# The flow layer's first stage put in batch order, its weights issued by the scalar engine, its first table load on a constant

## The chip, the cores and the metric

The kernel runs on one NeuronCore of a Trainium2 chip. Its engines are TensorE (PE, matrix products; PEld is its weight load), VectorE (DVE), ScalarE (ACT), GpSimd (POOL) and SyncE (SP), which here only issues transfers. Each engine runs its own list of instructions in order, and they meet through semaphores. The metric is the device time of one execution in microseconds.

## The reference, cut to what matters

Two layers of attention and feed-forward work on 2 x 1024 tokens of width 128. What the change touches is the beginning of the first one, a "flow" attention with 16 heads of 8:

```
x = L0_attn_inputs                                # (2, 1024, 128)
u = layernorm(x)
q = sigmoid(u @ Wq + bq); k = sigmoid(u @ Wk + bk); v = u @ Wv + bv
normal   = 1, 2, ..., L
sink_in  = normal / sum_d((q + EPS) * (cumsum(k) + EPS))
src_out  = normal / sum_d((k + EPS) * (cumsum(q) + EPS))
cons_sink = sum_d((q + EPS) * (cumsum(k * src_out) + EPS)) / normal
cons_src  = clip(sum_d((k + EPS) * (cumsum(q * sink_in) + EPS)) / normal, -1, 1)
sink_alloc = sigmoid(cons_sink)
e = exp(cons_src); src_comp = e / cumsum(e) * normal
x = einsum(q * sink_in / normal, cumsum(k (x) (v * src_comp))) * sink_alloc
```

After it come the output projection, a feed-forward part, a gated attention (8 heads of 64), a second attention (16 heads of 8) and a layer of experts. None of these is edited.

## The kernel before, in words

The kernel is a chain of blocks; at the end of each block all engines meet. The change is inside one block of `flow_phase`, the first, called "mass" (lines 282 to 600), and every later block starts after it.

The 2048 tokens are cut into four quarters of 512 (`QUARTERS`), each of four tiles of 128; quarters 0 and 1 are batch 0, quarters 2 and 3 are batch 1 (`PERB` is 2). A quarter goes through these steps:

- SP loads it (L334), one transfer of 256 KB.
- DVE takes mean and variance of its tiles (`quarter_stats`, L106 and L109), ACT takes the root (`quarter_root`, L117), DVE takes the reciprocal and applies both (`quarter_norm`, L124 and L127).
- PE turns it so that channels lie in the partitions (L466, four transposes against the constant `ident`).
- ACT copies the turned quarter as its high part (`quarter_high`, L144), DVE subtracts for the low part (`quarter_low`, L148).
- PE projects it (`project(m, q)`, m = 0, 1, 2 for q, k, v), three matmuls for each (L71 to L73), and ACT adds the bias and takes the sigmoid into `qT`, `kT` or `vT` (`activate`, L554). `PROJ` (L315) numbers the twelve projections; a projection waits until the one four before it was read.

POOL splits the weights into high and low parts (L156, L158) once all three have landed. From line 426 on DVE runs one long chain in which each instruction waits for the one before it (`done`, L362): running sums (`scan`, L371), products (`weigh`, L374), and shares by head. The head sums (L481) and their spreading back (L491) are small matmuls, the batches taken in turn. `fill` (L76) issues matmuls of the identity in bf16 whose result nobody reads.

The order on each engine is written out by hand. On PE (L495 to L505) and on ACT (L557 to L572) it is: batch 0 turned, its k and q projected, batch 1 turned, its k and q, then the four v. On DVE the statistics of a quarter, the norm of the one before and the low part of the one before that alternate (L414 to L421).

Of the kernel before, what the change touches and what calls it, by code (L numbers as in the profile page):

```python
# [64 lines left out]
def tile(t):  # L65
    return slice(t * P, (t + 1) * P)
# [184 lines left out]
def flow_phase(nc, psum, X, C, io, const, lead):  # L251
# [9 lines left out]
    with ExitStack() as ctx:  # L261
# [20 lines left out]
        with ExitStack() as ctx1:  # L282
# [7 lines left out]
            small = p1.sb("small", [P, 1])  # L290
            q_more, k_more = p1.sb("q_more", [P, SEQ]), p1.sb("k_more", [P, SEQ])
# [10 lines left out]
            x_loaded = [p1.sem(f"x_loaded{q}") for q in range(QUARTERS)]  # L302
            ident_loaded, w_loaded, bias_loaded = p1.sem("ident_loaded"), p1.sem("w_loaded"), p1.sem("bias_loaded")
# [26 lines left out]
            def _(sp):  # L330
# [4 lines left out]
                for n, name in enumerate(("Wq", "Wk", "Wv")):  # L335
                    sp.dma_start(w_raw[:, tile(n)], io[f"L0_attn_{name}"]).then_inc(w_loaded, 16)
                sp.dma_start(C["ident"], const["ident"]).then_inc(ident_loaded, 16)
# [21 lines left out]
            def _(dve):  # L359
# [31 lines left out]

                def allot(b):

                    dve.wait_ge(alloc_ready, b + 1)
                    done(dve.tensor_tensor(r_sink[:, b, :], r_sink[:, b, :], alloc[:, b, :], ALU.mult))
                    dve.wait_ge(exp_ready, b + 1)
                    done(dve.tensor_tensor_scan(cum_give[:, b, :], give[:, b, :], give[:, b, :], 0.0, ALU.add, ALU.bypass), f"cum_give{b}")
                    done(dve.tensor_tensor(give[:, b, :], give[:, b, :], normal[:, :], ALU.mult))
# [15 lines left out]
                for q in range(QUARTERS):  # L414
                    dve.wait_ge(x_loaded[q], 16)
                    norm.quarter_stats(dve, q)
                    if q >= 1:
                        norm.quarter_norm(dve, q - 1)
                    if q >= 2:
                        turn.quarter_low(dve, q - 2)  # L420
                norm.quarter_norm(dve, QUARTERS - 1)  # L421
                dve.wait_ge(ident_loaded, 16)
                dve.tensor_copy(C["ident_bf"], C["ident"])
# [23 lines left out]
                done(dve.tensor_scalar(give[:, 0, :], scratch[:, 0, :], 1.0, -1.0, ALU.min, ALU.max), "give0")  # L447
                dve.wait_ge(summed, 7)
# [6 lines left out]
                compete(0)  # L455
                allot(1)
# [5 lines left out]
            def _(pe):  # L462
# [31 lines left out]

                pe.wait_ge(ident_loaded, 16)  # L495
                for b in range(BATCH):
                    for q in range(b * PERB, (b + 1) * PERB):
                        turn_quarter(q)
                    if b == 0:
                        pe.wait_ge(lo_ready, 1)  # L500
                    for m in (1, 0):
                        for q in range(b * PERB, (b + 1) * PERB):
                            project(m, q)
# [22 lines left out]

                unused = [psum[:, 4 * b + 1, :] for b in range(BATCH)]
# [22 lines left out]
            def _(act):  # L550
# [5 lines left out]

                norm.quarter_root(act, 0)  # L557
# [6 lines left out]
                for b in range(BATCH):  # L564
                    if b:
                        for q in range(b * PERB, (b + 1) * PERB):
                            turn.quarter_high(act, q)
                    for m in (1, 0):
                        for q in range(b * PERB, (b + 1) * PERB):
                            activate(m, q)  # L570
# [21 lines left out]
            def _(pool):  # L592
                split_weights(pool, [(w_raw[:, :], w_hi[:, :], w_lo[:, :], 16 * 3)], w_loaded, hi_ready, lo_ready)
                pool.memset(v_one[:, :, :], 0.0)
# [2197 lines left out]
```

## Time and profile before

| | us |
|---|---|
| device time, median of 3 runs | 1154.37 (1152.71 to 1156.15) |
| the profiled execution, device time | 1154.81 |
| its span in the trace | 1153.0 |
| of it PE busy | 1078.8 (94%) |
| DVE busy | 899.2 (78%) |
| ACT busy | 712.9 (62%) |
| POOL busy | 406.7 (35%) |
| first block of the flow layer | 0 to 70 |

The busy shares are for the whole execution. The block that is edited is its first 70 us, and there the shares are quite different, so views of short stretches are what to read. Times in the rows are from the start of the span. In a row of the timeline the first number is the start, the second how long the instruction or the merged group (x4) took; in brackets stands how long its engine had been idle and what ended that.

### The profile page before, as it was taken

To read this page: it belongs to the slowest core of one execution; us is meant where nothing else is said; L and a number is where in the kernel's file an instruction comes from. 1 tells how busy PE (TensorE), PEld (TensorE's weight loads), DVE (VectorE), ACT (ScalarE), POOL (GpSimd) and SP (SyncE) were. 2 spreads that over 40 slices of the span, in tenths; PEclk is the share of its full clock that TensorE was granted. 3 is DMA by queue.
4 is the path that set the end of the run, shared out by engine and by line. 5 is a ranking of instruction groups with operands and counts; after the bars stand their busy time and mean duration, and the time that the engine had idled before them with its cause. 6 is when DMAs were issued, how large, how long until landed. Compare 5 with 4: busy or idle time off the path is not lost. (4 is left out here: it accounts for less than half of the span.)

```text
span 1153.0 us, 18898 instructions
## 1 busy us (share of the span) xinstructions
PE 1078.8 (94%) x7015; PEld 543.0 (47%) x7015; DVE 899.2 (78%) x1574; ACT 712.9 (62%) x1212; POOL 406.7 (35%) x256
## 2 busy tenths in 40 slices
PE   5499999999999999999989999999999899999997
PEld 4256675445454445545423222222212267888885
DVE  7968467866666767667788999999999268787777
ACT  5324557433334464533267888888888778888874
POOL 0137611867677776778522100000010011221200
PEclk9599999999999999999999999999999999999998
DMA  4000100000000000100010111000010012212101
GB/s 99 1 1 3 38 1 1 1 11 1 1 1 2 2 1 1 57 28 1 2 45 31 41 43 28 16 18 25 15 21 1 1 38 82 86 68 97 38 37 37
DMA packets 30916, 29.44 MB, mean 26 GB/s; under 512 B 10913, under 2 KB 26537, under 8 KB 29801
## 3 DMA queue, kind: packets, MB, share of 16 engines
q1 hardware_dynamic: 30824, 28.23, 8.4%
q8 instruction: 56, 0.92, 0.3%
q14 instruction: 36, 0.29, 0.1%
HBM read 23.57 MB, written 4.26 MB: 24 GB/s over the span
## 5 line engine op out<-in xcount | busy, mean ns | idle before, releaser
L1401 POOL TENSOR_TENSOR lead_room<-lead_room 128x1024 f32<-128x1024 f32 x112 | 269.1, 2402 | 116.5 <-ACT lead_room L1662 108.6
L2152 ACT ACTIVATE narrow_att_probs<-psum 128x512 f32<-128x512 f32 x512 | 264.7, 603 | 53.1 <-PE psum L2068 52.8
L2190 DVE TENSOR_REDUCE front_maxima<-psum 128x1 f32<-128x1024 f32 x240 | 281.7, 1219 | 15.6 <-PE psum L1164 10.8
L1662 ACT ACTIVATE lead_room<-psum 128x1024 f32<-128x1024 f32 x128 | 124.1, 1021 | 152.3 <-PE psum L1547 152.2
L1760 DVE TENSOR_REDUCE gated_maxima<-psum 128x1 f32<-128x512 f32 x256 | 164.5, 685 | 44.2 <-PE psum L1438 42.8
L2068 PE MATMUL psum<-narrow_att_q,narrow_att_k 50*128 50x512 bf16 x448 | 146.9, 384 | 3.8 <-ACT narrow_att_probs L2152 3.3
L1164 PE MATMUL psum<-narrow_att_k,narrow_att_q 48*128 48x512 bf16 x448 | 132.6, 381 | 9.6 <-DVE front_maxima L2190 2.8
L2081 PE MATMUL psum<-narrow_att_probs,narrow_att_v_ones 128*32 128x512 f32 x1024 | 137.1, 607 | 0.1
L2658 DVE TENSOR_TENSOR moe_hidden_lo<-moe_hidden,moe_hidden_hi 128x512 fp32r<-128x512 f32 x144 | 104.4, 751 | 39.2 <-ACT moe_hidden_hi L2567 38.7
L1560 PE MATMUL psum<-lead_room,gated_values 128*64 128x512 f32 x512 | 132.1, 610 | 0.0
L2563 ACT ACTIVATE moe_hidden<-psum,back_up_bias 128x512 f32<-128x512 f32 x144 | 96.2, 689 | 32.8 <-PE psum L73 32.8
L1164 PEld LDWEIGHTS psum<-narrow_att_k,narrow_att_q 48*128 48x128 bf16 x448 | 25.0, 94 | 145.5 <-DVE front_maxima L2190 135.8
L2567 ACT ACTIVATE moe_hidden_hi<-moe_hidden 128x512 fp32r<-128x512 f32 x144 | 87.0, 633 | 0.0
L1438 PE MATMUL psum<-gated_high 64*128 64x512 f32 x256 | 58.8, 456 | 8.1 <-DVE gated_maxima L1760 4.7
L1988 POOL COPY narrow_att_v_ones<-narrow_att_values 128x256 f32<-128x256 f32 x4 | 1.6, 400 | 160.9 <-PE psum L2081 160.9
L2068 PEld LDWEIGHTS psum<-narrow_att_q,narrow_att_k 50*128 50x128 bf16 x448 | 32.8, 93 | 46.9 <-ACT narrow_att_probs L2152 44.4
L1547 PE MATMUL psum<-gated_high 64*128 64x512 f32 x256 | 53.0, 398 | 0.0
L1547 PE MATMUL psum<-gated_high,gated_low 64*128 64x512 f32 x256 | 52.1, 390 | 0.0
L1547 PE MATMUL psum<-gated_low,gated_high 64*128 64x512 f32 x256 | 52.0, 389 | 0.0
L1560 PEld LDWEIGHTS psum<-lead_room,gated_values 128*64 128x64 f32 x512 | 28.7, 135 | 45.9 <-issue 43.8
L1751 DVE TENSOR_TENSOR gated_low<-psum,gated_high 128x512 fp32r<-128x512 f32 x32 | 22.1, 691 | 32.8 <-ACT gated_high L1618 32.8
L2408 POOL CAST moe_up_hi<-moe_raw_up 128x512 fp32r<-128x512 f32 x4 | 3.4, 861 | 122.8 <-DVE moe_UL L148 89.7
(401 smaller groups left out, 1918.1 us busy)
## 6 DMA issues: line engine op xcount, KB each, us to landing
moe_mixb<-moe_mix_scratch SPq DMA_DIRECT2D x8, 1024.0 KB, 5.1
narrow_parts_scratch<-gated_values SPq DMA_DIRECT2D x12, 128.0 KB, 2.1
narrow_parts_scratch<-narrow_att_part SPq DMA_DIRECT2D x12, 128.0 KB, 2.2
narrow_att_q<-narrow_parts_scratch SPq DMA_DIRECT2D x14, 96.0 KB
narrow_att_q<-narrow_parts_scratch SPq DMA_DIRECT2D x42, 32.0 KB
narrow_att_k<-narrow_parts_scratch SPq DMA_DIRECT2D x14, 96.0 KB
narrow_att_k<-narrow_parts_scratch SPq DMA_DIRECT2D x42, 32.0 KB
X<-in_L_attn_inputs SPq DMA_DIRECT2D x4, 256.0 KB, 4.0
```

The source lines that it names most:

```text
L1164: return pe.matmul(out, self.stack(0, n // 2)[64 * a:64 * a + self.ROWS, n % 2, r, tile(qt)], self.stack(1, n // 2)[64 * a:64 * a + self.R ...
L1401: pool.tensor_tensor(tally[:, n % 2, :, :], probs[:, kt % 4, :, :], so_far, ALU.add).then_inc(tallied, 1)
L1547: last = pe.matmul(psum[:, 2 * e + j, :], k[rows, b, 1, tile(2 * c + e)], q[rows, b, 0, cols], start=False, stop=(s == 2), skip_group_chec ...
L1560: last = pe.matmul(psum[DH * j:DH * j + DH, SUM_BANK, :], values[:, t, c0:c0 + DH], probs[:, kt % 4, j, :], start=(kt == 0), stop=(kt == S ...
L1662: act.activation(probs[:, k % 4, :, :], psum[:, 2 * e:2 * e + 2, :], ACT.Exp, scale=SCALE).then_inc(exped, 1)
L1760: dve.tensor_reduce(maxima[:, n % 2, x, at:at + 1], psum[:, bank, :], AX.X, ALU.max).then_inc(job_used, 1)
L2068: pe.matmul(psum[:, SCORE_BANK + j % 3, :], ks(n // 2, kt // QT, e)[rows, tile(kt % QT)], qs(n // 2, n % 2, e)[rows, :], start=True, stop= ...
L2081: last = pe.matmul(psum[32 * j:32 * j + 32, SUM_BANK, :], v_ones[:, n // 2 % 2, kt, j, :], probs[:, (n * STILES + kt) % 3, j, :], start=(k ...
L2152: act.activation(probs[:, k % 3, 2 * e + u % 2, :], psum[:, SCORE_BANK + j % 3, :], ACT.Exp, scale=SCALE).then_inc(exped, 1)
L2190: dve.tensor_reduce(maxima[:, n % 2, at:at + 1], chunk.rearrange("p a b -> p (a b)"), AX.X, ALU.max).then_inc(chunk_used, 1)
L2563: act.activation(hidden[:, k % 2, a, :], psum[:, a, :], ACT.Gelu, bias=up_bias[:, e, a:a + 1]).then_inc(hidden_ready, 1)
L2658: dve.tensor_tensor(hidden_lo[:, k % 2, a, :], hidden[:, k % 2, a, :], f32(hidden_hi[:, k % 2, a, :]), ALU.subtract).then_inc(hidden_lo_re ...
```

## The change

1. ACT issues the three weight transfers (Wq, Wk, Wv) as its first instructions, where SP had issued them behind the four quarters.
2. SP issues the identity after the second quarter, where it had come after all quarters and weights.
3. Before its first real root, ACT takes a root of a constant into an unread column (`unread`), so that the table load comes with that.
4. DVE takes the statistics of quarters 0 and 1, then norms 0 and 1, then statistics of 2, low part of 0, statistics of 3, low part of 1, then norms 2 and 3.
5. The bf16 copy of the identity is made by POOL and not by DVE, after the split of the weights. POOL's memset of `v_one`, which came behind the split, comes first.
6. PE waits for that copy, runs two fills, and one more after each of the turns of quarters 0 and 1. Then it projects k of batch 0, turns quarters 2 and 3, projects q of batch 0, and k and q of batch 1. ACT's order follows.
7. The product of `r_sink` and `alloc` (L395) is taken out of `allot` and stands as `gate`: for batch 0 right after `give0`, for batch 1 where it had been.

```diff
                 for q in range(QUARTERS):
                     part = slice(q * PER_Q, (q + 1) * PER_Q)
                     sp.dma_start(X[:, part, :], x_in[:, part, :]).then_inc(x_loaded[q], 16)
-                for n, name in enumerate(("Wq", "Wk", "Wv")):
-                    sp.dma_start(w_raw[:, tile(n)], io[f"L0_attn_{name}"]).then_inc(w_loaded, 16)
-                sp.dma_start(C["ident"], const["ident"]).then_inc(ident_loaded, 16)
+                    if q == 1:
+                        sp.dma_start(C["ident"], const["ident"]).then_inc(ident_loaded, 16)
...
+                def gate(b):
+
+                    dve.wait_ge(alloc_ready, b + 1)
+                    done(dve.tensor_tensor(r_sink[:, b, :], r_sink[:, b, :], alloc[:, b, :], ALU.mult), f"gated{b}")
+
                 def allot(b):
 
-                    dve.wait_ge(alloc_ready, b + 1)
-                    done(dve.tensor_tensor(r_sink[:, b, :], r_sink[:, b, :], alloc[:, b, :], ALU.mult))
...
-                for q in range(QUARTERS):
+                for q in range(PERB):
                     dve.wait_ge(x_loaded[q], 16)
                     norm.quarter_stats(dve, q)
-                    if q >= 1:
-                        norm.quarter_norm(dve, q - 1)
-                    if q >= 2:
-                        turn.quarter_low(dve, q - 2)
-                norm.quarter_norm(dve, QUARTERS - 1)
-                dve.wait_ge(ident_loaded, 16)
-                dve.tensor_copy(C["ident_bf"], C["ident"])
+                for q in range(PERB):
+                    norm.quarter_norm(dve, q)
+                for q in range(PERB):
+                    dve.wait_ge(x_loaded[PERB + q], 16)
+                    norm.quarter_stats(dve, PERB + q)
+                    turn.quarter_low(dve, q)
+                for q in range(PERB):
+                    norm.quarter_norm(dve, PERB + q)
...
+                gate(0)
                 dve.wait_ge(summed, 7)
...
                 compete(0)
+                gate(1)
                 allot(1)
...
                 pe.wait_ge(ident_loaded, 16)
-                for b in range(BATCH):
-                    for q in range(b * PERB, (b + 1) * PERB):
-                        turn_quarter(q)
-                    if b == 0:
-                        pe.wait_ge(lo_ready, 1)
-                    for m in (1, 0):
-                        for q in range(b * PERB, (b + 1) * PERB):
-                            project(m, q)
+                pe.wait_ge(bf_ready, 1)
+                fill(pe, C, unused[1], 2)
+                for q in range(PERB):
+                    turn_quarter(q)
+                    fill(pe, C, unused[1], 1)
+                pe.wait_ge(lo_ready, 1)
+                for q in range(PERB):
+                    project(1, q)
+                for q in range(PERB, QUARTERS):
+                    turn_quarter(q)
+                for q in range(PERB):
+                    project(0, q)
+                for m in (1, 0):
+                    for q in range(PERB, QUARTERS):
+                        project(m, q)
...
+                for n, name in enumerate(("Wq", "Wk", "Wv")):
+                    act.dma_start(w_raw[:, tile(n)], io[f"L0_attn_{name}"]).then_inc(w_loaded, 16)
+
+                act.wait_ge(norm.eps_ready, 1)
+                act.activation(unread[:, :], norm.eps[:, 0:1], ACT.Sqrt)
...
                 act.wait_ge(bias_loaded, 16 * 3)
-                for b in range(BATCH):
-                    if b:
-                        for q in range(b * PERB, (b + 1) * PERB):
-                            turn.quarter_high(act, q)
-                    for m in (1, 0):
-                        for q in range(b * PERB, (b + 1) * PERB):
-                            activate(m, q)
+                for q in range(PERB):
+                    activate(1, q)
+                for q in range(PERB, QUARTERS):
+                    turn.quarter_high(act, q)
+                for q in range(PERB):
+                    activate(0, q)
+                for m in (1, 0):
+                    for q in range(PERB, QUARTERS):
+                        activate(m, q)
...
+                pool.memset(v_one[:, :, :], 0.0)
                 split_weights(pool, [(w_raw[:, :], w_hi[:, :], w_lo[:, :], 16 * 3)], w_loaded, hi_ready, lo_ready)
-                pool.memset(v_one[:, :, :], 0.0)
+                pool.wait_ge(ident_loaded, 16)
+                pool.tensor_copy(C["ident_bf"], C["ident"]).then_inc(bf_ready, 1)
```

## Rows read from the trace of the kernel before

**Rows 1.** Busy time by stretch: length, busy us of PE, PEld, DVE, ACT, POOL; clock, DMA share, GB/s.
```profile
0.00:17.00 17.00, 5.92 (x17) 4.25 (x18) 11.40 (x58) 5.99 (x10) 2.65 (x7) 1.00 0.59 130
...
27.00:60.00 33.00, 17.11 (x209) 9.59 (x202) 31.39 (x29) 13.21 (x15) 4.71 (x2) 0.59 0.00 1
```

**Rows 2.** Timeline of the first 22 us, DVE.
```profile
3.79 0.88 DVE L106 BATCH_NORM_STATS2 flow_mass_norm_stats<-X 128x6 f32<-128x128 f32 x4 [2.89 <-DMA X<-in_L_attn_inputs]
4.86 0.84 DVE L106 BATCH_NORM_STATS2 flow_mass_norm_stats<-X 128x6 f32<-128x128 f32 x4
6.65 0.18 DVE L124 RECIPROCAL flow_mass_norm_rstd<-flow_mass_norm_std 128x4 f32<-128x4 f32 x1 [0.68 <-ACT flow_mass_norm_std L117]
7.89 0.87 DVE L106 BATCH_NORM_STATS2 flow_mass_norm_stats<-X 128x6 f32<-128x128 f32 x4
9.14 1.90 DVE L127 TENSOR_SCALAR flow_U<-X,flow_mass_norm_moments,flow_mass_norm_rstd 128x128 f32<-128x128 f32 x4
10.96 0.68 DVE L148 TENSOR_TENSOR lead_UL<-psum,lead_UH 128x512 fp32r<-128x512 f32 x1
11.56 0.86 DVE L106 BATCH_NORM_STATS2 flow_mass_norm_stats<-X 128x6 f32<-128x128 f32 x4
16.97 2.29 DVE L371 TENSOR_TENSOR_SCAN flow_mass_cum<-flow_kT 128x1024 f32<-128x1024 f32 x1 [1.09 <-ACT flow_kT L554]
20.37 1.29 DVE L148 TENSOR_TENSOR lead_UL<-psum,lead_UH 128x512 fp32r<-128x512 f32 x2 [1.11 <-ACT lead_UH L144]
21.57 1.22 DVE L374 SCALAR_TENSOR_TENSOR flow_mass_prod<-flow_qT,flow_mass_cum 128x1024 f32<-128x1024 f32 x1
```

**Rows 3.** Timeline of SP's first issues, of POOL and of ACT, until 18 us.
```profile
0.74 2.10 SPq L334 DMA_DIRECT2D X<-in_L_attn_inputs  x4
5.02 1.28 ACT L117 ACT_TABLE_LOAD   x1 [5.02 <-DVE flow_mass_norm_moments L109]
7.86 0.50 POOL L156 CAST flow_mass_w_hi<-flow_mass_w_raw 128x384 fp32r<-128x384 f32 x1 [7.42 <-DMA flow_mass_w_raw<-in_L_attn_Wv]
8.45 1.00 POOL L158 TENSOR_TENSOR flow_mass_w_lo<-flow_mass_w_raw,flow_mass_w_hi 128x384 fp32r<-128x384 f32 x1
9.38 1.01 POOL L594 MEMSET flow_v_one<- 128x1088 f32 x1
16.25 0.69 ACT L554 ACTIVATE flow_kT<-psum,flow_columns 128x512 f32<-128x512 f32 x1 [0.69 <-PE psum L73]
```

**Rows 4.** Timeline, PE, until 27 us.
```profile
8.13 1.08 PE L466 MATMUL psum<-ident,flow_U 128*128 128x128 f32 x4 [8.13 <-DMA ident<-const_ident]
14.56 0.79 PE L71 MATMUL psum<-lead_UH,flow_mass_w_hi 128*128 128x512 f32 x1 [1.07 <-DVE lead_UL L148]
17.29 0.63 PE L71 MATMUL psum<-lead_UH,flow_mass_w_hi 128*128 128x512 f32 x1
18.57 1.57 PE L466 MATMUL psum<-ident,flow_U 128*128 128x128 f32 x8
21.93 0.39 PE L71 MATMUL psum<-lead_UH,flow_mass_w_hi 128*128 128x512 f32 x1
22.62 0.39 PE L71 MATMUL psum<-lead_UH,flow_mass_w_hi 128*128 128x512 f32 x1
26.82 1.08 PE L481 MATMUL psum<-flow_mass_prod,flow_mass_sums_w 128*32 128x128 f32 x32
```

**Rows 5.** Transfers of the first 22 us: issuer, KB each, us to landing.
```profile
X<-in_L_attn_inputs SPq DMA_DIRECT2D x4, 256.0 KB, 4.0
```

**Rows 6.** Timeline of the later DVE chain, three rows, and PE's last head sums.
```profile
28.73 0.96 DVE L379 RECIPROCAL flow_mass_r_src<-psum 128x128 f32<-128x128 f32 x1
53.83 0.29 DVE L449 TENSOR_TENSOR flow_mass_take<-psum,flow_mass_inv_normal 128x128 f32<-128x128 f32 x1 [0.69 <-PE psum L481]
58.99 0.29 DVE L395 TENSOR_TENSOR flow_mass_r_sink<-flow_mass_r_sink,flow_mass_alloc 128x128 f32<-128x128 f32 x1
59.01 0.65 PE L481 MATMUL psum<-flow_mass_prod,flow_mass_sums_w 128*32 128x128 f32 x16 [0.18 <-DVE flow_mass_prod L374]
```

More of the change, by code:

```diff
@@ L290, in flow_phase @@
             small = p1.sb("small", [P, 1])
+            unread = p1.sb("unread", [P, 1])
             q_more, k_more = p1.sb("q_more", [P, SEQ]), p1.sb("k_more", [P, SEQ])
@@ L302, in flow_phase @@
             x_loaded = [p1.sem(f"x_loaded{q}") for q in range(QUARTERS)]
+            bf_ready = p1.sem("bf_ready")
             ident_loaded, w_loaded, bias_loaded = p1.sem("ident_loaded"), p1.sem("w_loaded"), p1.sem("bias_loaded")
@@ L493, in spread @@
                     last.then_inc(spreaded, 1)
+                unused = [psum[:, 4 * b + 1, :] for b in range(BATCH)]
                 pe.wait_ge(ident_loaded, 16)
-                for b in range(BATCH):
-                    for q in range(b * PERB, (b + 1) * PERB):
-                        turn_quarter(q)
-                    if b == 0:
-                        pe.wait_ge(lo_ready, 1)
-                    for m in (1, 0):
-                        for q in range(b * PERB, (b + 1) * PERB):
-                            project(m, q)
+                pe.wait_ge(bf_ready, 1)
[13 more added lines that the diff above has]
+                        project(m, q)
                 for q in range(QUARTERS):
@@ L525, in _ @@
                 spread(1, sink)
-                unused = [psum[:, 4 * b + 1, :] for b in range(BATCH)]
                 pe.wait_ge(step, AT["p1_2"])
```

## The prediction

> **What bounds the kernel now.** The edit lies in one block, so I read stretches first and then the timeline of that block, engine by engine. Over the whole span PE is busy 94%, but not here: in the first 17 us it is busy for 5.92 us, DVE for 11.40, and from 27 to 60 us DVE for 31.39 of 33 [rows 1]. The reader is to see that the block has two parts. From 21.57 on DVE runs a chain of products, running sums and reciprocals back to back; its one pause of weight is 0.69 us at 53.83, where it waits for a head sum [rows 2, 6]. Whatever brings the row at 21.57 forward brings the end of the block forward by as much, and all later blocks with it, since they start at the meeting point and are unchanged. Before 21.57 DVE has three pauses after its first instruction: 0.68 us for ACT's root, which stood behind a table load of 1.28 us; 1.09 for the sigmoid of k; and 1.11 for the high part of quarter 2 [rows 2, 3]. A fourth loss is hidden in a duration: the four norm instructions of quarter 1 took 1.90 us at 9.14, while the next two DVE rows after the norm of quarter 0 show that it took from 6.65 to 7.89 with its reciprocal. Beside the slow one POOL ran a tensor_tensor and the memset of 1.01 us [rows 2, 3]. PE starts at 8.13, when the identity lands, and runs at the lower of its two clock levels: one projection to the next takes 18.57 - 17.29 = 1.28 us, later 22.62 - 21.93 = 0.69 [rows 4]. The column of the granted clock says 1.00 for this stretch [rows 1]; the pace, 512 columns in 1.28/3 = 0.43 us, is that of 1.2 GHz, and I go by the pace.
>
> **The sum, for DVE.** Pieces, each with its overlap taken off: statistics of a quarter 4.86 - 3.79 = 1.07; norm 7.89 - 6.65 = 1.24; low part 11.56 - 10.96 = 0.60 [rows 2].
>
> *When norm 0 starts.* Before, the statistics of quarters 0 and 1 end at 6.65 - 0.68 = 5.97. The table load now lies in the first 4 us: three issues, by SP's 2.10 us for four, and the load are about 0.75 + 3 x 0.53 + 1.28 = 3.6 [rows 3], the constant's root ends before 4.0, and the root of quarter 0 then costs what is left, some 0.3 us, beside the statistics of quarter 1. So that pause goes. But 192 KB of weights and 64 KB of identity now travel with the first two quarters. The first quarter is used at 3.79, and DVE is waiting for it [rows 2]. The last one is issued at 0.74 + 2.10 x 3/4 = 2.3 and should land near 6.3, by the median of 4.0 us of the four [rows 3, 5]: three quarters in 2.5 us, some 300 KB/us. Bounds for the delay: 0, if the weights only fill gaps; and 192 KB at that pace, 0.64. I take 0.6 for the two statistics together, nearer the upper end, since the weights' first packets start with the first quarter's. Norm 0 then starts at 6.6 (5.97 to 6.65). The removed pause of 0.68 is thus nearly all paid back at the wires.
>
> The Trainium skill (DMA: Bandwidth & Descriptors, "Issuing engines are not separate DMA queues") says that transfers issued by different engines run on the same 16 DMA engines and that a second issuer saves only issue time. It speaks against part 1 of the change: by it alone the delay would be the upper 0.64 for quarter 0 and the forecast 0.05 us later; no row of before shows two issuers.
>
> *To the first scan.* Four norms, two statistics, two low parts: 4 x 1.24 + 2 x 1.07 + 2 x 0.60 = 8.30. 6.6 + 8.3 = 14.9. The slow norm's excess is left out because POOL's memset has moved to the start and the split of the weights falls beside statistics: weights issued by 2.2 us should be in by 4.8 to 5.5, and CAST, tensor_tensor and the copy end 1.9 us later, 6.7 to 7.4. The tail may lie on norm 0. The bounds are 0 and the 0.8 that the same collision cost before (from 9.14 to 10.96 is 1.82, against 1.24 less 0.2 for the reciprocal) [rows 2]; I take 0.2, since at most the last piece overlaps. The bf16 copy, on DVE before (0.22 us, hidden in the pause of 1.09), costs DVE nothing. Scan at 15.1 if k is ready.
>
> *Is k ready?* PE: copy ready about 7.0; two fills at 0.43 to 7.9, as U of quarter 0 comes (6.6 + 1.24 = 7.85, hence the fills cost nothing up to there); turn 1.1 to 9.0, fill 0.43, turn to 10.6, fill to 11.0. High part 0 is needed by DVE at 10.15 and is there at 9.7; high part 1 by 11.8 and is there at 11.3. Low part 1 is done at 12.5, projection of it 0.9 (fast) or 1.7 us (slow, as from 14.56 to 16.25 now [rows 3, 4]), sigmoid 0.69: 14.1 or 14.9; the first k also has the sigmoid's table load (1.28) before it and ends at 14.0 or 14.8, which moves the second to 14.7 or 15.5. So with the fast clock DVE never waits for k, with the slow one 0.4 us.
>
> *The clock.* Before, PE was unbroken from 14.56, after a gap of 1.07, and sped up between 17.29 and 18.57 [rows 4]. In the new order it has work from 7.0 on with gaps under 0.7 us; the same 4 us put the rise at about 11. I take the higher level (2.4 GHz) from there.
>
> *From the scan to the row at 21.57.* Running sum 2.3, two low parts 1.2: 15.1 + 3.5 = 18.6. The pause of 1.11 goes, since turn 3 needs only U of quarter 3 (15.1), ends at 15.9, is high at 16.6, and DVE asks at 17.4. q is projected from 15.9, at 0.69 each, done 17.4 and activated 18.1; DVE asks at 18.6. 21.57 - 18.6 = **3.0 us gained**.
>
> *Behind it.* The running sum of k of batch 1 (before from 28.73 - 2.3 = 26.4 [rows 6], now 23.4) needs k at once; PE projects it from 18.0, done by 20. The four v follow at 0.69 each and end near 23.5, before the head sums are wanted (26.82 before, 23.8 now) [rows 4]. The order within batch 1 and v has not changed.
>
> **gate.** L395 runs at 58.99 in the chain, and the next row starts 0.33 later (its 0.29 and the step's overhead). Put behind `give0` it fills the 0.69 pause before 53.83 [rows 6]; its input was made from `take0`, ten microseconds earlier. The cumulative sum, the carry and the head sum of 59.01 on PE are then just in time: PE's last head sums end at 59.66 [rows 6], DVE would ask at 59.8. **0.3 gained** (0 to 0.33). gate for batch 1 stands where it stood: 0.
>
> Costed at nothing: ACT's issues (1.5 us, before its first work at 5.02 [rows 3]); were the cover gone they would push the root. The later bias columns, constants and rows are issued about 2 us earlier by SP, the weights no longer being ahead of them. New waits: PE's on the copy has only turns and projections behind it; POOL's on the identity only the copy.
>
> **Sum.** 3.0 + 0.3 = 3.3 us off the profiled execution: 1154.81 - 3.3 = 1151.5, span 1149.7. It ran 0.44 above the median of 1154.37, so for the median I say **1151.1**. This kernel's measurement tells 0.3%, 3.5 us, from no change; the forecast lies just inside.
>
> **The rivals.**
> - *The wires cost nothing and POOL does not collide.* For it: the DMA share of the first 17 us is only 0.59 [rows 1]. Against: X is moved in a burst. Norm 0 at 6.0, scan at 14.3, gain 3.6 + 0.2 + 0.3 = 4.1: 1150.3.
> - *Late weights.* PE waits for POOL's copy, and that for all three weights. Were they as late as now (7.86 [rows 3]), the copy would be there at 7.86 + 1.9 = 9.8, fills to 10.6, turn to 11.7, high 12.4, where DVE wanted it at 10.1: 2.3 lost of 3.3. 1153.4. Half of that, 1152.2, is as likely. Against: ACT issues them by 2.3, when SP is only at its fourth quarter and has them still before it.
> - *The fills do not raise the clock early*, and it rises only near 18 as before. k 0.4 later; turn 3 ends 16.2, q of batch 0 is done at 19.0 and activated at 19.7 where DVE asks at 18.6: 1.1 to 1.3 lost, 1152.3. For it: one gap of about half a microsecond before each of U 2 and U 3.
> - *The clock stays low through v: slower than before.* The new order has waits between short pieces of PE work, where the old one had unbroken work from 14.56. Then the eight projections from 18.7 on at 1.28 end at 28.9, the head sums of batch 0, queued behind them, at about 31.2, where DVE used their result at 28.73 [rows 4, 6]: +2.5, less 0.3 of gate, 1156.6. It decides from the point where v ends after 26.7. Against: before, a gap of about 1 us before 21.11 left the pace high.
>
> **Chances.** Forecast 0.50; nothing on the wires 0.16; late weights 0.16; late clock 0.12; low through v 0.06. Range: from a microsecond under 1150.3, for what the late part and the runs' own spread (3.4 us over three) can add, to 1153.9, behind late weights: 1149.3 to 1153.9. Faster by over 0.3% (under 1150.9): nearly all of the second case and about half of the forecast, 0.41. Within: the rest of it and most of the two middle ones, 0.53. Slower by over 0.3%: 0.06.
>
> **What would show it.** In the new timeline: first statistics at 3.8 to 4.4; norm 0 at 6.6 with no idle before; no norm above 1.4 us; POOL's copy by 7.4; transposes and projections at the faster pace from about 11; first scan near 15.1, the first product (L374) at 18.6 with no idle time; v ended by 24; no pause over 0.4 at 53.8 less 3; the block's end 3.3 earlier. I am wrong if the statistics start after 4.6, if the copy comes after 8, if PE's pace at 16 us is still 1.28, or if later blocks do not simply shift.

## The result

The changed kernel takes 1152.40 us (median of 21 runs, 1149.87 to 1155.01) against 1154.67 for the kernel before (21 runs, 1152.49 to 1158.46), the ratio 0.9972, with a 95% interval from 0.9963 to 0.9980. Times the median that stood with the forecast, 1154.37, that is 1151.1. The gain, 3.2 us (2.3 to 4.3), is clear of zero, and its middle lies just inside the 0.3% that the prediction took as no change. A second session, of 12 runs against 23, gave 0.9959 (0.9947 to 0.9972), which is 4.7 us (3.2 to 6.1). The profiled execution has a span of 1150.3 us, against 1153.0 before and 1149.7 forecast.

**The profile after.** First the two stretches that answer to [rows 1], columns as there.

```profile
0.00:17.00 17.00, 8.48 (x32) 5.26 (x32) 12.97 (x57) 8.36 (x15) 2.94 (x8) 1.00 0.72 146
27.00:60.00 33.00, 18.45 (x218) 10.21 (x219) 31.28 (x36) 11.11 (x14) 3.28 (x2) 0.64 0.00 0
```

In the first 17 us DVE is busy for 12.97 instead of 11.40, PE for 8.48 instead of 5.92. Next the timeline of DVE in the front, to be laid beside [rows 2].

```profile
3.93 0.87 DVE L106 BATCH_NORM_STATS2 flow_mass_norm_stats<-X 128x6 f32<-128x128 f32 x4 [3.03 <-DMA X<-in_L_attn_inputs]
5.03 0.87 DVE L106 BATCH_NORM_STATS2 flow_mass_norm_stats<-X 128x6 f32<-128x128 f32 x4
...
6.10 0.14 DVE L124 RECIPROCAL flow_mass_norm_rstd<-flow_mass_norm_std 128x4 f32<-128x4 f32 x1
6.28 1.46 DVE L127 TENSOR_SCALAR flow_U<-X,flow_mass_norm_moments,flow_mass_norm_rstd 128x128 f32<-128x128 f32 x4
...
7.86 1.11 DVE L127 TENSOR_SCALAR flow_U<-X,flow_mass_norm_moments,flow_mass_norm_rstd 128x128 f32<-128x128 f32 x4
...
9.95 0.66 DVE L148 TENSOR_TENSOR lead_UL<-psum,lead_UH 128x512 fp32r<-128x512 f32 x1
...
14.76 2.29 DVE L372 TENSOR_TENSOR_SCAN flow_mass_cum<-flow_kT 128x1024 f32<-128x1024 f32 x1
17.09 1.29 DVE L148 TENSOR_TENSOR lead_UL<-psum,lead_UH 128x512 fp32r<-128x512 f32 x2
18.29 1.21 DVE L375 SCALAR_TENSOR_TENSOR flow_mass_prod<-flow_qT,flow_mass_cum 128x1024 f32<-128x1024 f32 x1
```

All three pauses that the prediction counted in [rows 2] are gone: between 3.93 and 18.29 no row of DVE names one. The first product starts 21.57 - 18.29 = 3.28 us earlier. The rest of the front's engines stand beside [rows 3, 4]:

```profile
2.16 1.28 ACT L575 ACT_TABLE_LOAD   x1 [2.16 <-issue]
5.31 0.50 POOL L156 CAST flow_mass_w_hi<-flow_mass_w_raw 128x384 fp32r<-128x384 f32 x1 [3.57 <-DMA flow_mass_w_raw<-in_L_attn_Wv]
5.89 0.99 POOL L158 TENSOR_TENSOR flow_mass_w_lo<-flow_mass_w_raw,flow_mass_w_hi 128x384 fp32r<-128x384 f32 x1
6.83 0.29 POOL L617 CAST ident_bf<-ident 128x128 bf16<-128x128 f32 x1
7.26 1.01 PE L80 MATMUL psum<-ident_bf 128*128 128x512 bf16 x2 [7.26 <-POOL ident_bf L617]
8.07 1.06 PE L473 MATMUL psum<-ident,flow_U 128*128 128x128 f32 x4
11.32 0.55 PE L72 MATMUL psum<-lead_UL,flow_mass_w_hi 128*128 128x512 f32 x1
11.70 0.39 PE L73 MATMUL psum<-lead_UH,flow_mass_w_lo 128*128 128x512 f32 x1
17.83 0.50 PE L71 MATMUL psum<-lead_UH,flow_mass_w_hi 128*128 128x512 f32 x1 [1.02 <-DVE lead_UL L148]
```

POOL has the weights at 5.31 instead of 7.86, the copy ends at 7.12, and a matmul of 512 columns goes from 0.63 to 0.39 us at 11.7: PE is at the higher level from there. Last, the places that answer to [rows 6].

```profile
25.45 0.96 DVE L380 RECIPROCAL flow_mass_r_src<-psum 128x128 f32<-128x128 f32 x1
49.89 0.29 DVE L396 TENSOR_TENSOR flow_mass_r_sink<-flow_mass_r_sink,flow_mass_alloc 128x128 f32<-128x128 f32 x1
50.54 0.29 DVE L455 TENSOR_TENSOR flow_mass_take<-psum,flow_mass_inv_normal 128x128 f32<-128x128 f32 x1 [0.36 <-PE psum L488]
55.71 0.42 DVE L401 TENSOR_TENSOR_SCAN flow_mass_cum_give<-flow_mass_give 128x128 f32<-128x128 f32 x1
65.15 1.22 DVE L414 TENSOR_TENSOR flow_vT<-flow_vT,psum 128x1024 f32<-128x1024 f32 x1 [1.89 <-PE psum L498]
```

The gate stands in the pause, of which 0.36 is left. The last product of the block starts at 65.15; in the trace of before the same instruction started at 68.74:

```profile
68.74 1.22 DVE L410 TENSOR_TENSOR flow_vT<-flow_vT,psum 128x1024 f32<-128x1024 f32 x1 [1.89 <-PE psum L491]
```

Its pause of 1.89 us is the longest of DVE's chain, and the prediction, which called the one at 53.83 the only one of weight, passed over it. It is the same before and after, since PE there spreads what DVE made just before, so it shifts with the chain. So **3.59 us are won in the block, but only 2.7 in the span**. Where the rest goes shows when the same DVE instruction is looked up in both traces: the distance is 3.8 us up to here,

```profile
172.24 0.16 DVE L208 RECIPROCAL lead_norm_rstd<-lead_norm_std 128x4 f32<-128x4 f32 x1
...
177.52 0.18 DVE L208 RECIPROCAL lead_norm_rstd<-lead_norm_std 128x4 f32<-128x4 f32 x1 [0.42 <-ACT lead_norm_std L117]
```

which before were, also in blocks that the change does not touch,

```profile
176.04 0.17 DVE L208 RECIPROCAL lead_norm_rstd<-lead_norm_std 128x4 f32<-128x4 f32 x1
...
180.44 0.18 DVE L208 RECIPROCAL lead_norm_rstd<-lead_norm_std 128x4 f32<-128x4 f32 x1
```

3.80 at the first pair, 2.92 at the second. Between them stands this, first the changed kernel, then the same work before (columns as in rows 1):

```profile
172.10:175.40 3.30, 3.30 (x10) 2.08 (x8) 3.27 (x12) 2.07 (x6) 1.17 (x1) 0.50 0.01 5
```

```profile
176.00:179.00 3.00, 2.92 (x13) 1.72 (x11) 2.97 (x10) 1.87 (x5) 1.07 (x1) 1.00 0.01 3
```

The granted clock was at 0.50 in the changed kernel, 1.00 before. Later the distance settles at 3.1, and past 590, where both traces have a fall of the clock, at 2.6 to 2.8. Whether the change is the cause is taken up below.

### The profile page after: what moved, and what is told of

It is laid out like the page before. It is cut to its first block and busy times, and to the rows that moved or that the text cites. A ratio compares the mean times of both kernels' runs of the same rounds, so it can differ in the third digit from the quotient of the medians.

```text
span 1150.3 us, 18908 instructions
## 1 busy us (share of the span) xinstructions
PE 1077.8 (94%) x7019; PEld 542.0 (47%) x7019; DVE 897.5 (78%) x1573; ACT 713.2 (62%) x1213; POOL 408.0 (35%) x257
## 5 line engine op out<-in xcount | busy, mean ns | idle before, releaser
L2213 DVE TENSOR_REDUCE front_maxima<-psum 128x1 f32<-128x1024 f32 x240 | 281.4, 1218 | 16.2 <-PE psum L1187 11.7
```

Source lines behind the costliest of these rows:

```text
L2213: dve.tensor_reduce(maxima[:, n % 2, at:at + 1], chunk.rearrange("p a b -> p (a b)"), AX.X, ALU.max).then_inc(chunk_used, 1)
```

## The experiments

Each kernel is the changed one with one part altered, save for the second traces of both kernels, the gap-filled one and the tuned one. Part 2 of the change (the earlier identity) and the place of the bf16 copy in part 5 were not taken away by themselves. The traces don't all begin alike: with the edits the first quarter of X is used between 3.93 and 4.45. So I count from the start of the first statistics (S) and give three distances: to the first product, from it to the first cumulative sum of give, and from that to the last DVE product of the block. The expectations' "mark" is where that last one ends, 1.22 us after its start. Of the edited kernels only the changed one itself was traced twice.

| kernel | S | S to first product | to cumulative sum | to last product | S to last product |
|---|---|---|---|---|---|
| before | 3.79 | 17.79 | 37.74 | 9.42 | 64.95 |
| before, again | 3.85 | 17.50 | 37.74 | 9.41 | 64.65 |
| changed | 3.93 | 14.37 | 37.41 | 9.44 | 61.22 |
| changed, again | 4.45 | 14.20 | 37.41 | 9.71 | 61.32 |
| gate_back | 4.02 | 14.66 | 37.74 | 9.42 | 61.82 |
| no_early_fills | 4.07 | 14.58 | 37.41 | 9.77 | 61.76 |
| no_constant_root | 4.22 | 14.60 | 37.42 | 9.61 | 61.63 |
| memset_last | 4.14 | 14.84 | 37.41 | 9.91 | 62.16 |
| weights_by_sp | 4.29 | 16.70 | 37.42 | 9.73 | 63.85 |
| dve_order_back | 4.09 | 15.12 | 38.86 | 9.69 | 63.67 |
| pe_act_order_back | 3.94 | 14.22 | 38.85 | 9.44 | 62.51 |
| order_back_gap_filled | 4.06 | 15.02 | 37.42 | 9.44 | 61.88 |
| low_weights_late | 4.18 | 13.88 | 37.41 | 9.72 | 61.01 |
| tuned | 4.24 | 13.87 | 37.41 | 9.44 | 60.72 |

Two traces of one kernel differ by 0.2 to 0.3 us in the first column of distances; smaller differences there say nothing.

**The gate** (`gate(0)` moved from behind `give0` to right before `allot(0)`).

```diff
-                gate(0)
                 dve.wait_ge(summed, 7)
...
+                gate(0)
                 allot(0)
```

> The changed kernel with the product of r_sink and alloc for batch 0 put back to its old place, right before the cumulative sum of give. The mark for this and the other single-part kernels is the end of the block's last DVE product (69.96 us in the kernel before, 66.37 in the changed one). My sum: the product fills DVE's pause at 49.9, so without it the pause is 0.69 again and the mark 0.33 later, 66.7. Rival: PE's head sums and carry were the bound there, then the mark stays within 0.1.

The middle distance goes from 37.41 to 37.74, 0.33 as expected. The mark, 67.06, is later than the expected 66.7, since in this trace DVE also waited 0.33 for k: PE's faster pace came at 13.32 and not at 11.70, with nothing edited there. In every other kernel that keeps the gate and no new fall of the clock the distance is 37.41 or 37.42.

**The early fills.**

```diff
-                fill(pe, C, unused[1], 2)
                 for q in range(PERB):
                     turn_quarter(q)
-                    fill(pe, C, unused[1], 1)
```

> The changed kernel without the four early fills; PE still waits for the bf16 identity. My reason: the fills bring the clock up early, the pace is the higher one from 11.3 us. Without them PE has gaps of up to 0.6 us until 10.7 and is unbroken from there, so the faster pace should come near 14.7; k is then 0.4 late, q 0.5 at most: mark 66.8 to 67.0. Rival 1, the fills are not needed for it: mark within 0.1. Rival 2, the clock stays low through v: head sums queue behind v and the mark is over 2 us later.

First product 0.21 later (within what two traces differ by), last product 0.54. The faster pace came within the row of turns at 13.81, where the expectation had 14.7 and the changed kernel has 11.7, and DVE waits 0.33 for k, expected 0.4:

```profile
13.38 0.63 PE L73 MATMUL psum<-lead_UH,flow_mass_w_lo 128*128 128x512 f32 x1
13.81 1.69 PE L473 MATMUL psum<-ident,flow_U 128*128 128x128 f32 x8
15.25 0.48 PE L71 MATMUL psum<-lead_UH,flow_mass_w_hi 128*128 128x512 f32 x1
...
15.12 2.29 DVE L372 TENSOR_TENSOR_SCAN flow_mass_cum<-flow_kT 128x1024 f32<-128x1024 f32 x1 [0.33 <-ACT flow_kT L566]
```

The pace came at 11.56 and 11.70 in the two traces of the changed kernel, but gate_back, which keeps the fills, has 13.32 and the same wait of 0.33. So the fills can bring it forward by some 2 us and don't always; little hangs on it. The 0.33 in the tail is the clock at another place: the fifteen fills at 50.7 ran slowly for longer (5.79 us against 4.56), and DVE waited 0.38 for head sums. It shows in some kernels with no edit there, in the second trace of the changed kernel too (5.72 us, a wait of 0.32).

**DVE's order.**

```diff
-                for q in range(PERB):
-                    dve.wait_ge(x_loaded[q], 16)
-                    norm.quarter_stats(dve, q)
-                for q in range(PERB):
-                    norm.quarter_norm(dve, q)
...
-                for q in range(PERB):
-                    norm.quarter_norm(dve, PERB + q)
+                for q in range(QUARTERS):
+                    dve.wait_ge(x_loaded[q], 16)
+                    norm.quarter_stats(dve, q)
+                    if q >= 1:
+                        norm.quarter_norm(dve, q - 1)
+                    if q >= 2:
+                        turn.quarter_low(dve, q - 2)
+                norm.quarter_norm(dve, QUARTERS - 1)
```

> The changed kernel with DVE's old order of statistics, norms and low parts (statistics of a quarter, norm of the one before, low part of the one before that), all else as changed. DVE has the same work either way. Theory A, the order itself is worth little, the gain is from the pauses taken away by other parts: low part 1 ends at 13.2 instead of 12.2, k of batch 0 is ready at 14.9, mark 66.4 to 66.6. Theory B, batch order is what brings k forward: with PE's turns and fills spread further the clock rises late and k comes at 15.6 or later, mark 67.2 or more.

First product 0.75 later and last product 2.45: nearer to theory B, whose 67.2 or more the mark of 68.98 goes far beyond, since neither theory had the second part of the loss. k came late, as theory B has it (DVE waits 0.84 for it at 15.68; the faster pace came by 13.99), and then the middle distance grew by 1.45. The next kernel shows what that is.

**PE's and ACT's order.**

```diff
-                for q in range(PERB):
-                    project(1, q)
-                for q in range(PERB, QUARTERS):
-                    turn_quarter(q)
-                for q in range(PERB):
-                    project(0, q)
+                for m in (1, 0):
+                    for q in range(PERB):
+                        project(m, q)
+                for q in range(PERB, QUARTERS):
+                    turn_quarter(q)
```

(and the same on ACT).

> The changed kernel with PE's and ACT's old order for batch 0 (k and q projected and activated before quarters 2 and 3 are turned), early fills kept. Theory A, what I predicted with: turning 2 and 3 first is what removes DVE's pause of 1.11 for the high part: mark about 1 us later, 67.4. Theory B: with k and q of batch 0 done by 16.2 on ACT the high parts 2 and 3 are there at 16.8 and 17.4, just when DVE asks (17.1, 17.7), so nothing is lost: mark within 0.2 of 66.37.

Theory B is right on the front, which is no later (14.22): DVE does not wait for the high parts. The mark, 67.66, is still nearer to theory A's 67.4, but by luck, since the loss is in another place, by a mechanism that neither theory named: the middle distance is 38.85.

```profile
17.70 0.62 PE L71 MATMUL psum<-lead_UH,flow_mass_w_hi 128*128 128x512 f32 x1 [2.19 <-DVE lead_UL L148]
18.11 0.63 PE L72 MATMUL psum<-lead_UL,flow_mass_w_hi 128*128 128x512 f32 x1
...
26.18 0.96 DVE L380 RECIPROCAL flow_mass_r_src<-psum 128x128 f32<-128x128 f32 x1 [0.90 <-PE psum L488]
...
28.17 1.18 DVE L382 TENSOR_TENSOR flow_mass_src<-flow_mass_r_src,flow_mass_normal 128x128 f32<-128x128 f32 x1
```

PE had idled 2.19 us with its turns and q done, and its granted clock fell. The stretch from 18.0 to 21.4 (columns as in rows 1), here:

```profile
18.00:21.40 3.40, 3.40 (x9) 2.61 (x9) 3.37 (x3) 1.37 (x2) 0.00 (x0) 0.51 0.13 37
```

and in the changed kernel:

```profile
18.00:21.40 3.40, 3.40 (x16) 2.79 (x17) 3.37 (x3) 2.57 (x4) 0.00 (x0) 1.00 0.07 19
```

Sixteen matmuls against nine in the same time. The projections of batch 1 end late, so do v and the head sums behind them; DVE waits 0.90, and the product at 28.17 takes 1.18 instead of 0.64. Beside it POOL has a product of its own, which ends at 29.20; the DVE product ends 0.15 later, and in the changed kernel, where POOL's ends at 27.93, 0.14 later. The two are the 1.44. That is the mechanism of my slower rival, over one short fall and not up to the end of v. The changed order leaves PE idle for only 1.02 at that place.

**The same with the gap filled** (against the kernel just above).

```diff
                 for q in range(PERB, QUARTERS):
                     turn_quarter(q)
+                pe.wait_ge(activated, MADE[(1, PERB - 1)])
+                fill(pe, C, unused[1], 8)
```

> As pe_act_order_back (the old order of PE and ACT for batch 0), with eight fills put where PE there idled 2.19 us before the projections of batch 1. In that trace the clock fell to its lower level from 17.93 to 21.34 and from the first product to the first cumulative sum of give it took 38.85 us, in the changed kernel 37.41. If the idle time of PE is what lets the clock fall, it stays high here until about 28 and the stretch takes 37.4 again: last product 61.2 to 61.6 after the first statistics (62.5 there). Rival: the fall belongs to a chance phase or to the order itself, then the 1.4 us stay.

```profile
16.04 1.89 PE L80 MATMUL psum<-ident_bf 128*128 128x512 bf16 x8
18.62 0.50 PE L71 MATMUL psum<-lead_UH,flow_mass_w_hi 128*128 128x512 f32 x1 [0.69 <-DVE lead_UL L148]
18.95 0.40 PE L72 MATMUL psum<-lead_UL,flow_mass_w_hi 128*128 128x512 f32 x1
```

The clock is 1.00 from 18.0 to 21.4, and the middle distance is 37.42 again. So the fall came from PE's idle time. The other traces bear it out: at this place PE idled 1.81 us in dve_order_back, and there the clock fell too, and 0.69 to 1.32 us in the twelve traces in which it did not. (S to last product is 61.88, above the expected 61.6: in this trace the weights landed only at 6.09, and POOL's tensor_tensor cost the norm of quarter 0 more, as in the next kernels.)

**Weights issued by SP**, behind the four quarters and the identity; POOL and PE as in the changed kernel.

```diff
-                for n, name in enumerate(("Wq", "Wk", "Wv")):
-                    act.dma_start(w_raw[:, tile(n)], io[f"L0_attn_{name}"]).then_inc(w_loaded, 16)
+                for n, name in enumerate(("Wq", "Wk", "Wv")):
+                    sp.dma_start(w_raw[:, tile(n)], io[f"L0_attn_{name}"]).then_inc(w_loaded, 16)
```

> The changed kernel with the weight transfers issued by SP again, after the four quarters, and PE's wait for the copy kept. First statistics then start at the old 3.79 instead of 3.93 if the weights on the wires delay the first quarter. The weights land near 8.2, POOL's copy is done near 10.1, PE starts 2.8 later than now. My rival of late weights put at that 2.3 us lost: mark 68.7 (68.2 to 69.2). If DVE's own work covers PE, mark within 0.5 of 66.4.

```profile
8.20 0.57 POOL L156 CAST flow_mass_w_hi<-flow_mass_w_raw 128x384 fp32r<-128x384 f32 x1 [6.46 <-DMA flow_mass_w_raw<-in_L_attn_Wv]
8.85 0.99 POOL L158 TENSOR_TENSOR flow_mass_w_lo<-flow_mass_w_raw,flow_mass_w_hi 128x384 fp32r<-128x384 f32 x1
9.78 0.29 POOL L616 CAST ident_bf<-ident 128x128 bf16<-128x128 f32 x1
...
7.80 2.12 DVE L127 TENSOR_SCALAR flow_U<-X,flow_mass_norm_moments,flow_mass_norm_rstd 128x128 f32<-128x128 f32 x4
12.75 0.69 DVE L148 TENSOR_TENSOR lead_UL<-psum,lead_UH 128x512 fp32r<-128x512 f32 x1 [1.77 <-ACT lead_UH L144]
```

First product 2.33 us later than in the changed kernel. Late weights were priced at 2.3 in the prediction, and by this path: the copy ends at 10.07, and DVE stands 1.77 us before low part 0. (The mark, 69.36, is past the expected 69.2, as S was 0.36 late.) POOL's split now also lies beside norm 1, which takes 2.12 instead of 1.11, within the time that DVE would have waited anyway. Without the issue by ACT the block is only 0.8 to 1.1 us shorter than before (by the two traces of before). But the loss needs two parts of the change together: late weights, and PE's new wait for a copy that POOL makes behind the split of the weights. No run has late weights without that wait, so what the issue by ACT is worth alone is open.

How it brings the weights forward can be read from the issues of Wv, the last of the three, before and changed:

```profile
3.95 0.43 SPq L336 DMA_DIRECT2D flow_mass_w_raw<-in_L_attn_Wv  x1
...
1.67 0.45 ACTq L572 DMA_DIRECT2D flow_mass_w_raw<-in_L_attn_Wv  x1
```

It is issued 2.28 us earlier and used 2.55 us earlier: most of it is time in SP's list, where each of the six issues before it took about half a microsecond.

The other expectation of this run fell: with no weights beside the first quarters the first statistics start at 4.29, later than in the changed kernel.

**The root of a constant** taken out.

```diff
-                act.wait_ge(norm.eps_ready, 1)
-                act.activation(unread[:, :], norm.eps[:, 0:1], ACT.Sqrt)
```

> The changed kernel without the root of a constant on ACT; the table load then stands before the first real root. It runs from 5.1 to 6.4, the root ends at 6.7, norm 0 starts at 6.75 instead of 6.10. Theory A: the whole 0.65 goes through to the mark (end of the block's last DVE product, 66.37 in the changed kernel): 67.0. Theory B: part of it comes back, since POOL's tensor_tensor on the weights (5.89 to 6.88) then no longer lies beside norm 0, which took 1.46 us instead of 1.11: mark 66.7.

Theory B. DVE waits 0.63 until 7.08 for the root, but the norm of quarter 0 then takes 1.11 instead of 1.46; S to first product is 14.60, 0.23 to 0.40 over the two traces of the changed kernel. The mark, 67.07, reads like theory A's 67.0, but 0.29 of it is the later S and 0.17 the tail.

**POOL's memset last.**

```diff
-                pool.memset(v_one[:, :, :], 0.0)
...
                 pool.wait_ge(ident_loaded, 16)
                 pool.tensor_copy(C["ident_bf"], C["ident"]).then_inc(bf_ready, 1)
+                pool.memset(v_one[:, :, :], 0.0)
```

> The changed kernel with POOL's memset of v_one behind the split and the bf16 copy, so from 7.1 to 8.1, beside norms 0 and 1. Theory A: a POOL instruction of 1.0 us blocks one DVE tensor_scalar as it did before (the norm of quarter 1 took 1.90 instead of 1.11): mark 0.6 to 0.8 later than 66.37. Theory B: only POOL instructions that read block DVE, and the 1.90 was from the tensor_tensor: mark within 0.1.

```profile
6.50 2.06 DVE L127 TENSOR_SCALAR flow_U<-X,flow_mass_norm_moments,flow_mass_norm_rstd 128x128 f32<-128x128 f32 x4
```

```profile
6.14 0.99 POOL L158 TENSOR_TENSOR flow_mass_w_lo<-flow_mass_w_raw,flow_mass_w_hi 128x384 fp32r<-128x384 f32 x1
7.08 0.29 POOL L616 CAST ident_bf<-ident 128x128 bf16<-128x128 f32 x1
7.31 1.11 POOL L617 MEMSET flow_v_one<- 128x1088 f32 x1
```

Four tensor_scalars take 2.06 us where they take 1.11 with POOL at rest and 1.46 in the changed kernel. The sum alone would not show that it is the memset, since beside POOL's split without a memset it came to 2.12 in weights_by_sp. The single instructions of this trace do: the first lasts to 7.22, just past the tensor_tensor; the second takes its usual 0.33; the third starts at 7.39 and lasts 1.10 us, to 8.49, 0.08 after the memset ends. So the memset, which only writes, blocks as well. Theory A in kind; at the first product it cost 0.47 to 0.64 by the two traces of the changed kernel, expected 0.6 to 0.8. The trace agrees with the Trainium skill (SBUF — State Buffer, "Who interferes with whom"), by which a DVE instruction in a two-port mode and a POOL instruction exclude each other for their whole length; the page has tensor_scalar among those that can be in such a mode. One row does not fit it: POOL's copy of the identity, 7.08 to 7.37, lies beside the second tensor_scalar, which took no longer than usual.

**The low part of the weights after norms 0 and 1**, and the version built from what the runs had shown.

```diff
                 pool.memset(v_one[:, :, :], 0.0)
-                split_weights(pool, [(w_raw[:, :], w_hi[:, :], w_lo[:, :], 16 * 3)], w_loaded, hi_ready, lo_ready)
+                pool.wait_ge(w_loaded, 16 * 3)
+                pool.tensor_copy(w_hi[:, :], w_raw[:, :]).then_inc(hi_ready, 1)
                 pool.wait_ge(ident_loaded, 16)
                 pool.tensor_copy(C["ident_bf"], C["ident"]).then_inc(bf_ready, 1)
+                pool.wait_ge(hi_ready, 1)
+                pool.wait_ge(norm.normed, PERB * PER_Q)
+                pool.tensor_tensor(w_lo[:, :], w_raw[:, :], f32(w_hi[:, :]), ALU.subtract).then_inc(lo_ready, 1)
```

> The changed kernel with another order on POOL: high part of the weights, bf16 copy of the identity, then the low part of the weights only once norms 0 and 1 are done. If the 0.35 us that norm 0 takes over its usual 1.11 is the collision with POOL's tensor_tensor, it goes: norm 0's tensor_scalars take 1.1 us, the first scan starts at 14.4 and the mark is 0.3 earlier, 66.05. PE's fills start near 6.2 and the faster pace comes at about 10.3. Rival: k is ready only at 14.73 (sigmoid's table load), DVE waits for it and the mark stays within 0.1; then half or less is won.

```profile
6.53 1.11 DVE L127 TENSOR_SCALAR flow_U<-X,flow_mass_norm_moments,flow_mass_norm_rstd 128x128 f32<-128x128 f32 x4
```

The norm of quarter 0 takes 1.11, the first scan starts at 14.54, though S is 4.18, and the first product comes 13.88 after S instead of 14.37 and 14.20. To the last product only 0.2 to 0.3 is won: the clock's place in the tail costs 0.3 in this trace, against the first of the changed kernel. The mark is 66.41 for the expected 66.05. The collision was worth 0.3 to 0.5 us. The tuned kernel adds:

```diff
-                fill(pe, C, unused[1], 2)
+                fill(pe, C, unused[1], 3)
...
+                fill(pe, C, unused[0], 4)
                 pe.wait_ge(step, AT["p1_2"])
                 head_sums(1, 2)
```

> The changed kernel with the low part of the weights made after norms 0 and 1 (as in the run before), three early fills instead of two, and four fills more while PE waits for the head sums of batch 1 near 47 us. Two reasons, each with its size: without the collision the row of the first product comes 0.45 to 0.5 us earlier, counted from the first statistics; and with PE unbroken from 45.8 the higher clock comes before the last head sums whatever the phase, so that from the first cumulative sum of give to the last product it takes 9.42 instead of up to 9.9. Last DVE product starts 60.7 after the first statistics (61.2 in the changed kernel's trace, 61.0 with low_weights_late). Device time 0.5 us under the changed kernel on the same chip. Rival: the four fills delay the head sums (they end at 48.8, head sums are due at 49.3; were they late, the mark would be later by that), or the later blocks' clock swamps it: no difference to the changed kernel beyond 0.5 us.

The block is as expected to the tenth, 60.72 from S to the last product, 0.5 shorter than the changed one. The whole is not: 1151.70 us (12 runs) against 1150.84 for the changed kernel on the same chip (12 runs), ratios to before 0.9963 (0.9950 to 0.9977) and 0.9959 (0.9947 to 0.9972). The 0.5 expected of the whole are not seen; the rival's second half holds: half a microsecond in the block can't be told in the whole, with these intervals.

**The two kernels again.**

> The changed kernel itself, timed on the same chip as the one above, with a second trace. If the mark depends on the phase of the clock only, the trace shows the first statistics between 3.9 and 4.3, and the last product starts 61.2 to 61.6 after them. The executions list granted clock and span of each: by the reason that falls of the clock to its lower level for 3.4 us at 128, 172 or later come in some executions and not in others, the span should fall by 1 to 1.5 us for each 0.0015 of mean clock. Rival: span and clock are unrelated, the 0.9 us given back behind 172 us belongs to the change.

> The kernel before, for a second trace. If the start of the first statistics (3.79 in the first trace, 3.93 to 4.29 in nine traces with the edits) is jitter of the transfers, it lies between 3.8 and 4.3 here; if the weights issued by ACT delay the first quarter, it is again under 3.85. From the first statistics to the last product: 64.95, as before, give or take 0.4 for the clock's phase.

S was 3.85 in the second trace of before, and 3.93 to 4.45 in the twelve others; the second trace of the changed kernel, at 4.45, lies outside what was expected of it (3.9 to 4.3). That looks like a delay by the weights, but the kernel without weights beside the first quarters has 4.29. There the identity still travels behind the second quarter, and no run takes that away. What sets S is open; at most 0.1 to 0.6 of it belongs to the edit.

Span and clock: of the changed kernel 33 executions have both on record, from two sessions. Mean clock runs from 0.979 to 0.985, span from 1153.2 to 1147.5, with a correlation of -0.85, and a straight line through them gives 1.0 us for 0.0015, at the lower end of the expected 1 to 1.5. In traces of one kernel the falls between the first block and the end do lie at different places: the first of the changed kernel has them at 128, 172 and 588 us, the second only at 588. The fall at 172, the 0.9 us given back, thus does not come with the change each time: of the twelve traces with edits one other, order_back_gap_filled, has it, and neither of before. At a clock of 0.983 the lines give 1149.8 for the changed kernel and 1153.2 for the one before (25 executions), 3.5 us apart, which is what the block says (counted from S, 3.7 and 3.3 by the two pairs of traces). Within the second session alone they are 4.0 apart (12 and 23 executions), and the medians 5.0. One thing may add to the block there: a fall near 130 us is in both traces of before and in four of the twelve with edits. Whether the change makes it rarer is not shown.

## Why the prediction was right

Forecast 1151.1 and 3.3 us; measured 3.2 (2.3 to 4.3) by the ratio, 3.59 in the block. The place and the main mechanism were right, DVE's pauses in the front and one chain behind them. That the ratio agrees to 0.1 us is partly luck: the block gave 0.3 more than forecast, the profiled pair 2.7, the second session 4.7. By its steps:

- **When norm 0 starts** (6.6). It started at 6.10, with S 0.14 later than before, so the term of 0.6 for the weights on the wires was over-sized for this trace; in the second trace S is 4.45 and norm 0 starts at 6.61, and the term fits. Nothing shows which part of that is the weights. The rule of the Trainium skill (DMA: Bandwidth & Descriptors, "Issuing engines are not separate DMA queues") that a second issuer only saves issue time agrees with the issues of Wv: 2.28 of the 2.55 us are earlier issue. By the page that time is "usually small relative to the DMA itself", which does not fit here (2.28 us beside 3.6 from issue to landing), and the prediction's sentence that the rule speaks against the issue by ACT misjudged it, because SP's list had the weights behind four quarters.
- **To the first scan** (8.3 + 0.2). It took 14.76 - 6.10 = 8.66, of which 0.35 is POOL's tensor_tensor beside norm 0, foreseen at that place with 0.2. ("No norm above 1.4 us", among what would show the forecast, did not hold: the four instructions of norm 0 alone took 1.46.) The rest, 8.31, is the sum of the pieces.
- **Is k ready, the clock.** Pace from 11.7, forecast about 11; the copy ended at 7.12, forecast 7.0. k and DVE were ready within 0.1 of each other at 14.7.
- **To the first product** (3.5). 18.29 - 14.76 = 3.53. Gained 3.28, forecast 3.0. The reason that I gave for the third pause failed: with the rest of the change in place DVE does not wait for the high part under the old PE order either (pe_act_order_back). The new order pays by keeping PE's idle time at 1.02 instead of 2.19, and so the clock up, which is worth 1.2 to 1.3 us at the last product. That this step came out right in size is luck.
- **gate** (0.3): 0.33, and gate_back gives it back.
- **Late blocks simply shift**: they do not, and the prediction had named that as a sign of being wrong. The clock's falls differ from one execution to the next; by the line above, the mean clock's range of 0.006 goes with some 4 us of span, more than the whole gain. Here that shook the number and not the mechanism in the block.
- **Rivals.** Late weights cost 2.33 when they were made late, priced at 2.3. The low clock through v did not come: PE idled 1.02 us before the projections of batch 1 and v, where 1.81 and 2.19 us stood before the falls of two other kernels, and even those lasted 3.4 us and not up to the end of v. The best case, 4.1, missed by the collision and by S.

## What to carry to other kernels

Where the span moves by more than the edit from one execution to the next, count the edit in its own block, from one instruction to another, in two traces of each kernel, and look at the granted clock before giving a later difference a cause. Before reordering PE, look at how long it idles between two pieces: here 0.7 to 1.3 us were free and 1.8 and 2.2 us lost 1.4 us, which showed on DVE only 8 us after the gap. On POOL ask for each instruction what DVE runs beside it: the work itself is off the path, its place cost 0.3 to 0.5 us. Before putting an instruction's wait on another engine, ask what that engine has to finish first: the copy behind the weights' split cost 2.3 us as soon as the weights were late.

## What was not expected of the hardware

A memset of 1.1 us on POOL, which reads nothing, held up a DVE tensor_scalar for its whole length: 1.10 us instead of 0.34, and four of them 2.06 instead of 1.46. The start of the first statistics, which only waits for one transfer of 256 KB, moved between 3.79 and 4.45 us from trace to trace. And in the first microseconds the column of the granted clock says 1.00 while matmuls of 512 columns start 0.43 us apart, the pace of 1.2 GHz, both before the change and after it.
